# Decoder layer: feed-forward products in fp32, eight gathers a batch, and gathers between the second batch's rows

## What is computed

```python
x = _layernorm(x + _L0_attn_ref(x, qkv_w, out_w, gate_w, norm_w))
x = _layernorm(x + _L0_xattn_ref(x, ctx_4096, ...))   # quantise both, matmul
x = _layernorm(x + _L0_ffn_ref(x, up, down, perm))
# _L0_ffn_ref, 16 heads of 64 values, 256 hidden ones each
t = x[:, perm].reshape(b * l, 16, 64)
t = gelu(einsum('bhd,hdm->bhm', t, up))               # up (16, 64, 256)
t = einsum('bhm,hmd->bhd', t, down)                   # down (16, 256, 64)
out = t.reshape(b * l, 1024)[:, argsort(perm)]
```

## Time and profile before

| | us |
|---|---|
| median of the runs | 2096.89 |
| profiled execution | 2101.18 |
| its span in the trace | 2099.3 |
| last transpositions of batch 0's rows | 1885.2 |
| last transpositions of batch 1's rows | 1958.4 |
| batch 0's last total, begin | 2009.6 |
| batch 1's last total, begin | 2076.3 |

### The profile page before, as it was taken

The page is one execution under the profiler, slowest core; times in us unless marked ns, Lnnn a source line. Parts: engine busy times, 40 slices in busy tenths (PEclk is TensorE's granted clock), DMA queues, the critical chain, the costliest instruction groups (busy, mean ns, idle before and its releaser), DMA issues.

```text
span 2099.3 us, 28487 instructions
## 1 busy us (share of the span) xinstructions
PE 1914.5 (91%) x10882; PEld 1043.3 (50%) x10889; DVE 1353.4 (64%) x1887; ACT 899.8 (43%) x1351; POOL 480.5 (23%) x390
## 2 busy tenths in 40 slices
PE   5889999999999999999999999999999999865654
PEld 4344646464646455555546464646464655432211
DVE  7476666757575757575756566565656565785787
ACT  4443434344343535252534343434434353344663
POOL 4212121212121203122121212121111110123455
PEclk9999999999999999999999999999999999987876
DMA  4112021212122212112120202121111214123311
GB/s 172 41 41 101 23 100 40 101 41 96 45 71 71 71 51 73 69 61 81 41 71 28 78 27 71 41 71 41 63 49 41 71 41 161 41 84 87 91 56 55
DMA packets 46390, 139.30 MB, mean 66 GB/s; under 512 B 3888, under 2 KB 12208, under 8 KB 43696
## 3 DMA queue, kind: packets, MB, share of 16 engines
q1 hardware_dynamic: 33376, 120.60, 17.0%
q0 software_dynamic: 3840, 12.59, 1.9%
q10 hardware_dynamic: 9040, 4.29, 0.7%
HBM read 124.88 MB, written 12.58 MB: 65 GB/s over the span
## 4 chain that ended last, share of the span: by engine, by line
PE 78%; DVE 11%; ACT 5%; issue 5%; POOL 1%; DMA 1%; POOLq 0%; ACTq 0%; DVEq 0%
PE bank L1090 18%; PE bank L1113 13%; PE bank L1114 13%; PE bank L1115 13%; PE bank L1130 5%; PE bank L1132 5%; PE bank L1131 5%; PE bank L1157 1%; PE bank L1155 1%; PE bank L1156 1%; DVE x_blocks L1563 1%; DVE bank L1488 1%; DVE gated_split L1568 1%; DVE bank L1503 1%; DVE w_pair L1395 1%
## 5 line engine op out<-in xcount | busy, mean ns | idle before, releaser
L1113 PE MATMUL bank<-x_blocks,w_pair 128*128 128x512 f16 x1344 | 512.1, 381 | 29.3 <-DVE bank L1432 11.3
L1115 PE MATMUL bank<-x_blocks,w_pair 128*128 128x512 f16 x1344 | 511.7, 381 | 0.0
L1114 PE MATMUL bank<-x_blocks,w_pair 128*128 128x512 f16 x1344 | 511.7, 381 | 0.0
L1090 PE MATMUL bank<-w_vo,gated_split 128*128 128x512 f16 x1440 | 324.1, 380 | 17.6 <-issue 13.8
L1130 PE MATMUL bank<-w_vo,x_blocks 128*128 128x256 f16 x1024 | 279.9, 273 | 12.4 <-DVE w_vo L1395 8.7
L1132 PE MATMUL bank<-w_vo,x_blocks 128*128 128x256 f16 x1024 | 279.8, 273 | 0.0
L1131 PE MATMUL bank<-w_vo,x_blocks 128*128 128x256 f16 x1024 | 279.8, 273 | 0.0
L1609 POOL TENSOR_TENSOR sums_pair<-raw_pair 128x512 f32<-128x512 f32 x48 | 68.2, 1421 | 902.3 <-DVE w_pair L1395 558.5
L1090 PEld LDWEIGHTS bank<-w_vo,gated_split 128*128 128x128 f16 x1440 | 140.0, 98 | 186.9 <-issue 16.9
L1113 PEld LDWEIGHTS bank<-x_blocks,w_pair 128*128 128x128 f16 x1344 | 132.0, 98 | 187.1 <-ACT gate_units L1297 15.5
L1115 PEld LDWEIGHTS bank<-x_blocks,w_pair 128*128 128x128 f16 x1344 | 131.9, 98 | 160.3 <-issue 3.0
(11 more groups left out here) (191 smaller groups left out, 2759.0 us busy)
## 6 DMA issues: line engine op xcount, KB each, us to landing
raw_pair<-w_qk SPq DMA_DIRECT2D x32, 1024.0 KB, 5.2
raw_pair<-w_v SPq DMA_DIRECT2D x16, 1024.0 KB, 4.9
raw_pair<-w_gate SPq DMA_DIRECT2D x16, 1024.0 KB, 4.9
raw_pair<-w_out SPq DMA_DIRECT2D x16, 1024.0 KB, 5.0
decay_sb<-decay SPq DMA_DIRECT2D x32, 256.0 KB, 5.2
raw_pair<-ctx_in SPq DMA_DIRECT2D x8, 1024.0 KB, 4.9
acc<-x_t SPq DMA_DIRECT2D x4, 1024.0 KB, 11.0
ctx<-raw_pair SPq DMA_DIRECT2D x8, 512.0 KB, 2.7
```

The lines of the kernel that those rows point to most:

```text
L1090: last = pe.matmul(out, a, b, start=m == 1, stop=m == n)
L1113: pe.matmul(bank[:, :], w_hi, x_hi, start=fresh and k == 0, stop=False, skip_group_check=not fresh)
L1114: pe.matmul(bank[:, :], w_hi, x_lo, start=False, stop=False, skip_group_check=not fresh)
L1115: mm = pe.matmul(bank[:, :], w_lo, x_hi, start=False, stop=k == QT - 1, skip_group_check=not fresh)
```

## The change

- The feed-forward weights are no longer split. Two loads (`ffn_load`) bring them as fp32 straight into the memory of `w_pair`; `load`, `step_loads`, `split` and the calls of `between()` go.
- A gather fetches 128 different rows, that is two heads: head 2p in partitions 0 to 63 and 2p+1 in 64 to 127, into `x2p`. There are eight a batch, and none waits for a spare buffer. `f_split` goes.
- `up` makes one fp32 product a head, over its 64 partitions and into a bank of its own. One Gelu a head writes fp32. `down` makes one fp32 product a head, in its column half. The addition to y is one instruction over 128 partitions.
- POOL adds sums for p = 0, 2, 4 alone. For p = 1, 3, 5, 6, 7 ACT squares and PE totals. The two banks of the totals are taken at p = 1 instead of 6.
- Order: after batch 0's rows, four steps of batch 1's rows, then eight times a gather and a row step, then two row steps to one of the feed-forward part (three to one before), then three feed-forward steps ahead of batch 1's gathers.

```diff
     def load_ffn_weights(self, free):
-        for i in range(4):
-            self.queue_load(self.extras, "ffn", ("up", 0, i), self.split_weight(free, done))
-        for i in range(2):
-            self.queue_load(self.extras, "ffn", ("down", 0, i), self.split_weight(free, done))
+        for name in ("up", "down"):
+            self.add("ffn_load", name=name, free=free)
+            self.ffn_w = self.tick("ffn_in", 16)
...
     def ffn_phase(self, b):
-        self.odd_queue.extend((b, 2 * p + 1) for p in range(FP))
+        got, hs, ys, t_y = {}, {}, {}, {}
         for p in range(FP):
-            self.gather(b, 2 * p, None, None)
-            self.gather_odd()
-        yield
+            self.add("gather", b=b, p=p, stored=list(self.x2_stored[b]), over=self.x2_over[b])
+            got[p] = self.tick(f"gathered{b}_{p}", 16)
+            yield
...
-            if p == 0:
+            if p == POOL_SUMS[0]:
                 self.add("sums_first", b=b, p=p, y=y, free1=free[0], free2=free[1])
                 free[:] = self.tick("sum1"), self.tick("sum_act")
-            elif p < FP - NLAST:
+            elif p in POOL_SUMS:
...
-                i = p - (FP - NLAST)
-                self.add("sums_last", b=b, p=p, i=i, y=y, free=self.sq_last_free[i])
+                i = p % 2 if p < FP - 1 else 0
+                self.add("square", b=b, p=p, i=i, y=y, free=self.sq_last_free[i])
...
     run((rows[0], 3), (rows[1], 1), until=lambda done: rows[0] in done)
-    plan.x2_in_free = [products_over, plan.x2_over[0]]
     ffn = [plan.ffn_phase(b) for b in range(B)]
-    next(ffn[0])
-    run((rows[1], 3), (ffn[0], 1), until=lambda done: rows[1] in done)
+    some(rows[1], 4)
+    for _ in range(FP):
+        next(ffn[0])
+        next(rows[1])
+    run((rows[1], 2), (ffn[0], 1), until=lambda done: rows[1] in done)
     plan.sum_free[1] = [plan.q1n_free[(0, 0)], plan.q1n_free[(0, 1)]]
-    next(ffn[1])
+    some(ffn[0], 3)
+    some(ffn[1], FP)
...
         elif kind == "up":
...
             for a in range(2):
-                bank, h = c.banks[st["banks"][a]], 2 * st["p"] + a
-                ms = slice(st["mc"] * P, (st["mc"] + 1) * P)
-                pe.matmul(bank[:, :], c.up_2[:, 0, h, ms], c.x_2[b][:, h, :], start=True, stop=False)
-                mm = pe.matmul(bank[:, :], c.up_2[:, 1, h, ms], c.x_2[b][:, h, :], start=False, stop=True)
-            mm.then_inc(sem["up_mm"])
+                rows, at = slice(a * FD, (a + 1) * FD), st["p"] * FM + st["mc"] * P
+                until(pe, sem, st["free"][a])
+                pe.matmul(c.banks[st["banks"][a]][:, :], c.up_sb[rows, at:at + P], c.x2p[b][rows, st["p"], :], start=True,
+                          stop=True).then_inc(sem["up_mm"])
         elif kind == "down":
...
-                pe.wait_ge(sem["h_lo"], st["h"][a][1])
-                pe.matmul(out, c.down_hl[:, 0, at, :], hid[:, 0, :], start=mc == 0, stop=False)
-                pe.matmul(out, c.down_hl[:, 0, at, :], hid[:, 1, :], start=False, stop=False)
-                pe.matmul(out, c.down_hl[:, 1, at, :], hid[:, 0, :], start=False, stop=mc == 1).then_inc(sem["down_mm"])
+                at = ((2 * p + a) * 2 + mc) * FD
+                pe.wait_ge(sem["gelu"], st["h"][a][1])
+                pe.matmul(bank[a * FD:(a + 1) * FD, :], c.down_sb[:, at:at + FD], c.hid[st["slots"][a]], start=mc == 0,
+                          stop=mc == 1).then_inc(sem["down_mm"])
...
-                act.activation(c.h_hl[st["slots"][a]][:, 0, :], ps, ACT.Gelu)
-                act.activation(ps, ps, ACT.Gelu).then_inc(sem["gelu"])
+                act.activation(c.hid[st["slots"][a]], c.banks[st["banks"][a]][:, :], ACT.Gelu).then_inc(sem["gelu"])
...
-                dve.tensor_tensor(y[0:FD], bank[0:FD, :], y[0:FD], ALU.add)
-                dve.tensor_tensor(y[FD:P], bank[FD:P, :], odd[FD:P], ALU.add).then_inc(sem["y"])
+                dve.tensor_tensor(y, c.banks[st["bank"]][:, :], y, ALU.add).then_inc(sem["y"])
```

More of the change, by code:

```diff
@@ L135, in add, with load @@
         return fields
-    def load(self, what):
+    def load(self, b, s):
         i, slot, free = self.raw.take()
-        self.add("load", what=what, slot=slot, free=free)
+        self.add("load", b=b, s=s, slot=slot, free=free)
         return i, self.tick(f"raw_in{slot}", 16)
[L144 to L170, removed]
-    def load_ffn_weights(self, free):
-        def done(token):
-            self.ffn_w = token
-        for i in range(4):
-            self.queue_load(self.extras, "ffn", ("up", 0, i), self.split_weight(free, done))
-        for i in range(2):
-            self.queue_load(self.extras, "ffn", ("down", 0, i), self.split_weight(free, done))
+    def load_ffn_weights(self, free):
+        for name in ("up", "down"):
+            self.add("ffn_load", name=name, free=free)
+            self.ffn_w = self.tick("ffn_in", 16)
     def stash_scale(self):
@@ L423, in rows_tile @@
         self.ring.give(i, st["var"])
-        j, landed = self.load(("xn", b, s))
+        j, landed = self.load(b, s)
         yield
@@ L577, in total @@
             i, p, y, sq = to_total.pop(0)
-            if i == 0:
+            first, last = not totals, p == FP - 1
+            if first:
                 totals.extend(self.ring.take() for _ in range(2))
-            last = i == NLAST - 1
-            self.add("total", b=b, p=p, i=i, y=y, sq=sq, last=last, banks=[t[1] for t in totals],
-                     free=[t[2] for t in totals] if i == 0 else [None, None], sums=list(self.sum_free[b]))
+            self.add("total", b=b, p=p, i=i, y=y, sq=sq, first=first, last=last, banks=[t[1] for t in totals],
+                     free=[t[2] for t in totals] if first else [None, None], sums=list(self.sum_free[b]))
             done[:] = self.tick("total_mm"), self.tick("total_mm")
             self.sq_last_free[i] = done[1]
-        split_x2(0)
-        split_x2(1)
-        yield
         for n in range(2 * FP + LAG):
@@ L808, in final_part @@
     late = plan.unsplit[0]["slot"]
-    def between(steps=1):
-        plan.step_loads(plan.extras, steps)
     def out(n, *js):
@@ L826, in run, with some @@
                             done.add(phase)
+    def some(phase, steps):
+        for _ in range(steps):
+            next(phase, None)
     plan.split_vo(0)
@@ L849, in final_part @@
     out(n, 0, 1, 2, 3)
-    between()
     out(n, 4, 5, 6, 7)
@@ L1262, in scalar_program @@
         b = st.get("b")
-        if kind == "split":
-            hi, _ = c.weight_target(st["what"])
-            src = c.raw[st["slot"]][:, 0:hi.shape[-1]]
-            act.wait_ge(sem[f"raw_in{st['slot']}"], st["landed"][1])
-            until(act, sem, st["free"])
-            act.activation(hi, src, ACT.Copy).then_inc(sem["w_hi"])
-        elif kind == "pair_split":
+        if kind == "pair_split":
             src, (hi, _) = c.pair_blocks(st["part"], st["slot"], st["wp"])
@@ L1399, in vector_program @@
         b = st.get("b")
-        if kind == "split":
-            hi, lo = c.weight_target(st["what"])
-            dve.wait_ge(sem["w_hi"], st["hi"][1])
-            split_low(c.raw[st["slot"]][:, 0:hi.shape[-1]], 1.0, hi, lo).then_inc(sem["w_lo"])
-        elif kind == "pair_split":
+        if kind == "pair_split":
             src, (hi, lo) = c.pair_blocks(st["part"], st["slot"], st["wp"])
```

153 lines of the change are left out of this document (39 added, 114 removed).

## The result

The changed kernel takes 2037.26 us (median of four runs, 2036.53 to 2038.20) against 2097.00 us of the kernel before beside it: ratio 0.9714, with a 95% interval from 0.9697 to 0.9731. It is 60 us faster; the prediction said 49, inside its range of 2030 to 2084. The profiled execution took 2038.20 us at a span of 2036.3.

The account below looks back on a forecast made before the run. No engine was full in the old end, a relay between ACT, DVE, POOL and PE; afterwards PE bounds it. Rows 1936 + products 77.8 + waits 14 + tail 22 = span 2050, plus 1.9 less 4.3: 2048 us, range 2030 to 2084.

Parts of the forecast that it names:

- restarts at half clock: After each of some four PE pauses behind the rows, products restart at half clock, 1.3 us lost each, 5 us together.
- Order: Batch 1's row steps ahead of and between batch 0's gathers: normalisation near 1895.7 instead of 1911.36, 15.7 us earlier.
- Rival 5: Batch 1's rows don't get ahead, the wait only moves: last transpositions near 1952, 16 later, 2064 us; chance 0.11.
- Pairs in fp32: Feed-forward steps: both heads' fp32 products run together, on row halves (up) and column halves (down), 0.95 us a step.
- Rivals 1 and 3: Fp32 pairs on row halves don't overlap, 2071 us, chance 0.11; no pairs overlap at all, 2097 us, chance 0.05.
- Rival 2: Strict program order in feed-forward steps: a pair overlaps by half only, 1.28 us instead of 0.85, 2073 us; chance 0.08.
- PE as the bound: Between batch 1's last transpositions and the last total PE sets the end, busy over 85%.
- Rival 4: PE works on at 1.2 GHz throughout, as pairs on parts of the array don't raise the clock: 2119 us; chance 0.07.
- The rows: Batch 1's last transpositions start at 1936 instead of 1958.4: 15.7, 5 and 2.5 us earlier, 1 later for gathers.
- The weights' 2.5 us: Six feed-forward weight splits go from DVE, three beside the start of batch 0's rows: 2.5 us saved (0 to 3.7).
- The products: PE behind batch 1's last transpositions: 58 steps 55.3 us, 24 totals 20.5, transpositions 2.0, together 77.8 us.
- The waits: PE pauses behind the rows: 5 us at batch 0's reciprocal, 4 at the last addition and totals, 5 for restarts; 14 together.

Follow-up runs that it names:

- experiment 1: Changed kernel with the order of before (all eight gathers of batch 0 right behind its rows, three row steps to one feed-forward step): 2043.11 us.
- experiment 9: Kernel before with the six splits of the feed-forward weights cut from 1024 columns to 8: 2097.01 us against 2097.66, ratio 0.9994.
- Experiment 2: Kernel before with the new order alone, keeping fp16 halves, sixteen gathers a batch and all splits: 2085.51 us, ratio 0.9936.
- Experiments 5: Changed kernel with the sums for p=1, 3 and 5 moved from PE's totals back to POOL: 2036.78 us, against 2037.26.
- experiment 6: Changed kernel with the sums of p=1 to 6 on DVE, eight fp32 totals a batch less on PE: 2023.66 us, ratio 0.9642.

## Why the prediction was right, and where its terms were off

Its main mechanism held: rows that run ahead, pairs that overlap, and PE as the bound behind them. Of its smaller terms the restarts at half clock didn't come. Where no experiment is named, the numbers below are from the profile of the kernel after.

- **Order.** Forecast: normalisation at 1895.7. Measured: 1894.89. Rival 5 (rows don't get ahead) is out. But the prediction put all of these 15.7 us down to the order and did not ask what it would be worth beside the other edit: undone alone it costs 6 us, and 9.3 of the 16.5 us at the normalisation come without it (experiment 1).
- **Pairs in fp32.** Forecast: both overlap, 0.95 us a step. Measured 1.06 and 1.01, against 1.91 and 1.86 when the overlap is taken away. Rivals 1 and 3 are out. Rival 2 wanted 1.28 or more for a step; the strict order that the Trainium skill gives ("TensorE: Matmul & The Clock Gate", part 3, "The mechanism") doesn't describe these pairs, though each product leaves two records.
- **PE as the bound.** Forecast: busy over 85%. Measured: 78.2 of 80 us (98%). The counts were exact: behind the last transpositions L1133 has 108 records (27 up steps), L1141 has 124 (31 down steps).
- **The clock.** Forecast: above 0.9. Measured: 1.00 from 1930 to 2010. Rival 4, the one that would have made the kernel slower, is out.
- **The tail.** 22.0 us forecast. PE's last total starts at 2013.32, lasts 1.02 and ends at 2014.3; the span ends 22.0 us later.

The 11 us between 2048 and 2037 come from these terms:

1. *The rows, 9.2 us too late* (1936 against 1926.79). The weights' 2.5 us are not shown: batch 0's last transpositions came 1.1 us earlier (1884.06 against 1885.2), and experiment 9 can't tell 2.5 us from nothing. The step that was off is the next one, from the normalisation to the last transpositions: 47.1 us before, 40.5 forecast (less 5 for splits and subtractions, less the 2.5, plus 1 for gathers, as the weights were put here), 31.9 measured. Experiment 2 divides it: with the new order and the old arithmetic it is 41.7 us (1896.56 to 1938.30), so the new order itself gives 5.4, and the arithmetic another 9.8, about twice the 5 that I had counted off the chain. I had counted only the splits that stood in the chain's rows. The window from the normalisation to the last transpositions, first in experiment 2 and then in the kernel after (columns as above), tells what the 9.8 us are:

```profile
1896.56:1938.30 41.74, 24.67 (x150) 12.70 (x151) 33.84 (x57) 29.27 (x43) 17.22 (x21) 0.92 0.40 114
```
```profile
1894.89:1926.79 31.90, 25.78 (x148) 12.22 (x149) 23.66 (x41) 20.92 (x27) 10.59 (x15) 0.89 0.35 99
```

   The granted clock is 0.92 in the longer of the two and 0.89 in the shorter, so the clock doesn't account for the 9.8 us. DVE is busy for 10.2 us less, ACT for 8.3 less and POOL for 6.6 less, while PE has 1.1 us more: what went is the work of the engines that hand over to PE. Which engine's share it was no run separates. The clock has its part in the other 5.4 us, those between the kernel before and experiment 2. In the kernel before the granted clock was 0.64 and 0.78 in the stages from 1886 to 1958, and two of its context products behind 1911 took 5.87 and 5.45 us:

```profile
1921.79 5.87 PE L1206 MATMUL bank<-x_blocks,k_units 128*128 128x512 bf16 x16 [1.80 <-DVE acc L1558]
...
1935.86 5.45 PE L1206 MATMUL bank<-x_blocks,k_units 128*128 128x512 bf16 x15 [1.40 <-DVE acc L1558]
```
```profile
1926.33 3.63 PE L1222 MATMUL bank<-x_blocks,k_units 128*128 128x512 bf16 x15 [0.51 <-DVE gated_split L1584]
```

   The last row is from experiment 2, where all four context products behind 1894 take 3.40 to 3.63 us. How much of the 5.4 us came by way of the clock no run separates.
2. *The products, about 5 us too short.* 58 steps at 0.95 were 55.3 us in the sum (55.1 by the product); at 1.06 and 1.01 they are 59.9. 24 totals at 0.85 were 20.5; from start to start they take 0.86 next to another total and 0.95 to 1.00 with a change of shape beside them, 22.7 in all. The transpositions took 1.0 us instead of 2.0. I had added 0.1 us for a step's change of shape, as the fp16 row showed; in fp32 it is 0.17.
3. *The waits, 14 forecast, some 4 measured.* From start to start the up step at 1971.73 took 3.55 us in its two parts instead of 1.06 (the reciprocal), the up step at 1928.82 1.94 instead of 1.06 (a y addition), the down step at 1988.04 1.54 instead of 1.01 (another), and the up step at 1976.29 1.56 instead of 1.06. The term that was off is above all the 5 us of restarts at half clock: the granted clock stayed at 1.00. I had assumed four pauses with a restart behind each; between the last transpositions and the last total the longest idle time was 1.37 us. Experiments 5 and 6 show that the restart itself was no mistake: behind 5.25 us, and behind two waits close together, the next products ran at half the clock.

Together: 9.2 earlier, then 87.5 us (1926.79 to 2014.3) instead of 91.8, 4.3 less. The span is 2036.3 instead of 2050, and the profiled execution stood 0.9 us above its median, not 4.3 (1.9 - 0.9 = +1.0 on the span instead of -2.4). That makes 2050 - 9.2 - 4.3 + 1.0, within a few tenths of 2037.3. In the second term there is some luck: products 5 us too short and waits 10 us too long cancel in half.

## What to carry to other kernels

Where a stage is a relay of engines that are each partly idle, an arithmetic that gives one engine less to hand over can be worth far more than its own instruction count: here PE had the same busy time and the end came 60 us earlier. Once that engine is full, read its timeline from start to start: what leaves it reaches the end (16 totals, 13.6 us), if the engine that takes it over keeps up; grouping steps of the same shape gave 4.5 us more for an edit of the order alone. Equal busy times don't mean equal work: look at the granted clock beside them. Two edits that shorten the same wait don't add (12 us alone, 6 beside the other), so price an order against the kernel with the other edits in it, not against the one before.

## What the runs showed of the hardware

- Two fp32 products of 512 columns on the two 64-row halves of the array, each into its own bank, take the time of one: 1.06 us against 1.91 on the same half. On two 64-column halves it is 1.01 against 1.86.
- A change between the two kinds costs 0.17 us: 4.13 us for four steps in turn, 3.79 grouped.
- From 1930 to 2010 us, all of it such pairs and full-array fp32 totals with 1.8 us of idle time, the granted clock was 1.00.
- An idle time of 1.37 us (1974.23) left the clock at full here, and so did one of 1.80 us (1926.79) with a wait of some 0.9 us inside the up step at 1928.82 soon after it. In experiment 6 waits of 0.45 and 1.39 us, 2.5 us apart, were followed by steps at half of it. What tells these cases apart stays open.
